# Row-tiled matmuls of an attention kernel, paired by pass: two scores side by side, then both halves of a maximum unit

## The reference

```python
xn = layernorm(x)
k, q, v = split(xn @ W_kqv.T)                      # 8 batches, 16 heads, 1024 tokens, 16 columns
score = einsum('bhsd,bhnd->bhsn', q, k) / 16 + bias
out_attn = softmax(score) @ v
result = x + out_attn + ffn(xn)
```

## Time and profile before

| what | value |
|---|---|
| time, median of 3 runs | 2495.86 us (2490.36 to 2496.33) |
| time of the profiled execution | 2484.07 us |
| its span | 2482.3 us |
| mean granted TensorE clock | 0.98 |
| busy: PE, DVE, ACT, POOL | 97%, 77%, 63%, 31% of the span |
| PE matmul instructions | 19286 |
| first maximum matmul, first score matmul | 1106.3 us, 1143.0 us |
| first score matmul of the last group | 2436.45 us |

### The profile page before, as it was taken

How to read it: one execution, slowest core, us unless ns; L and a number is a source line. 1 busy time by engine, 2 the same in 40 slices (tenths; PEclk the granted TensorE clock), 3 DMA queues, 4 the chain that set the end, 5 groups by cost and what they waited for, 6 DMA issues and landing times.

```text
span 2482.3 us, 53369 instructions
## 1 busy us (share of the span) xinstructions
PE 2396.7 (97%) x19286; PEld 1475.7 (59%) x19286; DVE 1910.9 (77%) x2905; ACT 1561.7 (63%) x3212; POOL 781.2 (31%) x901
## 2 busy tenths in 40 slices
PE   6999999994999999988999999999999999999998
PEld 5888888884999999973333333333333333333333
DVE  5666666656556555559999999999999999999994
ACT  3333333333333333324888888888888888888888
POOL 2223332224342222220113333333333333333333
PEclk9999999996999999987999999999999999999999
DMA  6999978880232222234434344343434353535331
GB/s 187 169 165 160 184 139 145 137 127 27 80 95 75 75 76 76 72 70 72 70 62 88 76 77 81 75 83 71 86 70 86 69 90 65 90 66 92 63 58 42
DMA packets 177922, 229.01 MB, mean 92 GB/s; under 512 B 42828, under 2 KB 127436, under 8 KB 177656
## 3 DMA queue, kind: packets, MB, share of 16 engines
q1 hardware_dynamic: 153048, 172.02, 38.6%
q0 software_dynamic: 22448, 50.56, 8.7%
q10 hardware_dynamic: 2176, 3.02, 0.3%
HBM read 131.47 MB, written 93.66 MB: 91 GB/s over the span
## 4 chain that ended last, share of the span: by engine, by line
PE 53%; DVE 1%; DMA 0%; ACT 0%; issue 0%; SPq 0%; DVEq 0%
PE p_o L1399 23%; PE p L1389 19%; PE p L1376 9%; PE p L1409 1%; DVE part L1231 1%; PE p L1382 1%; DMA q_op<-m_row 0%; ACT probs L1351 0%; ACT o_sb L1339 0%; SPq L1120 0%; DVE neg L1239 0%; DVE att L1258 0%; DVE att L1278 0%; DVE rec L1255 0%; DVEq L1224 0%
## 5 line engine op out<-in xcount | busy, mean ns | idle before, releaser
L1231 DVE TENSOR_REDUCE part<-p 128x2 f32<-128x1024 f32 x1024 | 1243.2, 1221 | 73.8 <-PE p L1376 66.7
L1351 ACT ACTIVATE probs<-p 128x512 f32<-128x512 f32 x2048 | 1112.6, 597 | 162.1 <-PE p L1389 131.0
L1376 PE MATMUL p<-k_op,q_op 50*128 50x512 f32 x2048 | 759.4, 462 | 13.9 <-DVE part L1231 10.9
L1389 PE MATMUL p<-q_op,k_op 51*128 51x512 f32 x2048 | 758.6, 452 | 0.9 <-DVE part L1231 0.4
L1399 PE MATMUL p_o<-probs,v_op 128*32 128x256 f32 x8192 | 655.5, 392 | 4.5 <-ACT o_sb L1339 0.8
L1389 PEld LDWEIGHTS p<-q_op,k_op 51*128 51x128 f32 x2048 | 311.2, 185 | 417.8 <-ACT probs L1351 374.3
L1399 PEld LDWEIGHTS p_o<-probs,v_op 128*32 128x32 f32 x8192 | 163.7, 108 | 359.3 <-ACT probs L1351 305.8
L1376 PEld LDWEIGHTS p<-k_op,q_op 50*128 50x128 f32 x2048 | 304.3, 189 | 29.4 <-DVE part L1231 26.2
L1182 POOL TENSOR_TENSOR att<-o_t,rec 128x256 f32<-128x256 f32 x63 | 39.0, 619 | 810.9 <-DVE rec L1247 810.9
L809 POOL DMA_INDIRECT xe<-xn_scratch,ids x135 | 144.4, 1070 | 361.4 <-DMA ids<-lists_scratch 345.6
L902 ACT ACTIVATE gated_e<-p_gate 128x352 f32<-128x352 f32 x135 | 62.6, 464 | 190.7 <-PE p_gate L840 190.7
(11 more groups left out here) (178 smaller groups left out, 4046.7 us busy)
## 6 DMA issues: line engine op xcount, KB each, us to landing
k_op<-qk_scratch SPq DMA_DIRECT2D x192, 128.0 KB
q_op<-qk_scratch SPq DMA_DIRECT2D x192, 128.0 KB
yr_scratch<-y SPq DMA_DIRECT2D x135, 128.0 KB, 1.7
qk_scratch<-k_op SPq DMA_DIRECT2D x32, 512.0 KB
qk_scratch<-q_op SPq DMA_DIRECT2D x32, 512.0 KB
v_scratch<-v_op SPq DMA_DIRECT2D x16, 1024.0 KB, 15.5
v_op<-v_scratch SPq DMA_DIRECT2D x32, 512.0 KB, 9.9
x<-in_x SPq DMA_DIRECT2D x16, 512.0 KB, 4.3
```

The source lines that it names most:

```text
L1231: v.tensor_reduce(part[c_ % 2][:, kh, :, qb], p1[use % 2][:], AX.X, ALU.max, negate=True).then_inc(s["s1_read"], 1)
L1351: a.activation(probs[kb % 4][:, h], p2[use % 3][:], ACT.Exp).then_inc(s["s2_read"], 1)
L1376: return t.matmul(p1[use % 2][:, x], q_op[u][lo:lo + S1_ROWS, pair, q0:q0 + P], k_op[u][lo:lo + S1_ROWS, pair, kh * 512:(kh + 1) * 512], s ...
L1389: t.matmul(p2[use % 3][:], k_op[u][lo:lo + S2_ROWS, pair, kb * P:(kb + 1) * P], q_op[u][lo:lo + S2_ROWS, pair, half * HQ:(half + 1) * HQ], ...
```

## The change

Both scores of a step are issued together at odd n, and behind them both halves of the maximum unit. No instruction is added or removed. The step becomes score(n-1), x=0 | score(n), x=1 | max_half x=0 | max_half x=1 | products. The score with x = 1 is now second in the order and the wait for it moves with it; the wait on `s1_read` moves from the head of the step to a place behind both scores. The prologue is left as it is.

```diff
@@ -1432,14 +1432,15 @@
                     if n == 0:
                         pe.wait_ge(v_in[u], (turn + 1) * 16)
                     use, use1 = use2(g, n), ring1(g) + n // 2
-                    pe.wait_ge(s["s2_read"], use + 1)
-                    if has_next and n % 2 == 0:
-                        pe.wait_ge(s["s1_read"], use1 + 1)
-                    score(u, use, n)
+                    if n % 2:
+                        for m in (n - 1, n):
+                            pe.wait_ge(s["s2_read"], use2(g, m) + 1)
+                            score(u, use2(g, m), m)
                     if has_next:
-                        ins = max_half(nu, use1, n // 2, 1 - n % 2)
                         if n % 2:
-                            ins.then_inc(s["s1_ps"], 1)
+                            pe.wait_ge(s["s1_read"], use1 + 1)
+                            max_half(nu, use1, n // 2, 0)
+                            max_half(nu, use1, n // 2, 1).then_inc(s["s1_ps"], 1)
                         if n == TURN_AT:
                             turn_max(g + 1, 0, use + 1)
                     if n == OWN_TURN:
```

## The result

| | median | runs |
|---|---|---|
| before | 2493.84 us | 5, 2490.36 to 2496.33 |
| after | 2506.55 us | 5, 2503.19 to 2510.34 |
| after / before | 1.0057 | 95% interval 1.0043 to 1.0071 |

The change costs 0.57%, some 14 us (the two medians differ by 12.7). It was predicted as 16.7 us on top of the kernel before (2512.6 us against a median of 2495.86), within 2491 to 2540.

The account below looks back on a forecast made before the run. The prediction took PE to bound the kernel, with DVE close behind. Terms of 14.6, 1.8 and about 0.3 us made 16.7 us on the median of 2495.86: 2512.6 us, range 2491 to 2540.

Parts of the forecast that it names:

- PE is the bound, so its loss counts in full: Attention: PE bounds the chain, so a slower PE adds its whole loss; a faster one gains at most 63 us.
- The pairing costs and gains nothing: Ordinary steps: score beside score, maximum beside maximum run like mixed pairs; 0, bounds 0.01 us a step either way.
- The first rival: All 992 steps: alternating order starts second pairs up to 0.10 us earlier, DVE then bounds; 2433 us; chance 0.08.
- The rule of the Trainium skill: Weight loads: one overlaps matmuls in flight only when its row group differs, favouring the new order; counted as 0.
- The late step: Step of l=6 and 7: second score waits for its buffer, products 0.24 us later, 61 times, 14.6 us.
- The step of l = 16 and 17: Step behind the output transpose: second score waits for the first exponential; 0.03 us, 61 times, 1.8 us.
- The slack of 0.06 us in ordinary steps: Ordinary steps: second score could start 0.06 us before the step does, so its earlier wait costs 0.
- the second rival: Ordinary steps lack the slack: exponential 0.03 us late in 930 steps, 28 us more, 2541 us; chance 0.13.
- The total: Whole kernel: the step losses together add 16.7 us, all on PE, giving 2512.6 us against the median.
- The 0.3 us for the first group: Second step of the first group: a buffer is waited for there too, about 0.3 us.
- only neighbours in the order pair up: Matmuls on the array: taken for granted that only neighbours in program order run side by side; no size given.

Follow-up runs that it names:

- the early transpose: Transpose of maxima moved from l=5 to behind the products of l=3: 2489.85 us on the kernel before, 2495.21 us on the changed kernel.
- the first four runs above: Changed kernel, old order at l=6,7: 2486.99 us; old order, second score's wait first: 2511.84; transpose of maxima at l=9: new order 2508.44, old order 2497.71.
- the first experiment: Changed kernel with the old order restored only in the step of l=6 and 7: 2486.99 us, 0.9986 of the kernel before.

## Why the prediction was right

*PE is the bound, so its loss counts in full.* It did: DVE's wait for PE grew by 15.3 us and attention by 17.0.

*The pairing costs and gains nothing.* Ordinary steps are 1.235 to 1.240 us, with the loads where they were forecast, 0.11 us into the step. The first rival (faster) needed loads that start sooner, and there were none to start sooner. The rule of the Trainium skill (TensorE: Matmul & The Clock Gate, Part 3, "What overlaps and what doesn't"), weighed in the prediction, would by the first rival's working have made a step up to 0.10 us shorter; no run here shows it. The run with both scores on one half goes against the rule: its second loads are on the rows of the matmuls in flight, and its step is 1.233 us all the same.

*The late step.* Predicted 0.24 us, measured 1.567 - 1.329 = 0.238. With 61 of them that is 14.5 us of the 17.0. Four runs bear on its cause: the wait alone, moved in the old order, brings it; the old order in that one step takes it away; a transpose in another place of the buffer ring makes it smaller; and the old waits with two matmuls left on the late score's rows bring it too.

*The step of l = 16 and 17.* Predicted 0.03, measured 0.021: 1.3 us instead of 1.8.

*What I had not counted.* Six single steps of the table's places l = 12, 13 and l = 0, 1 were longer by 0.17 to 0.69 us, 2.1 us in all, and one of l = 4, 5 by 0.16. In each that I looked at, ACT started an exponential late though its score was done. The longest:

```profile
1348.76 0.50 PE L1389 MATMUL p<-q_op,k_op 51*128 51x512 f32 x1
1349.45 0.50 PE L1389 MATMUL p<-q_op,k_op 51*128 51x512 f32 x1 [0.19 <-ACT probs L1351]
```

```profile
1348.80 0.60 ACT L1351 ACTIVATE probs<-p 128x512 f32<-128x512 f32 x1 [0.90 <-PE p L1389]
```

```profile
1348.88 1.23 DVE L1231 TENSOR_REDUCE part<-p 128x2 f32<-128x1024 f32 x1 [0.58 <-PE p L1376]
```

DVE started its reduction late at the same moment (its matmuls end at 1348.26), so it isn't ACT alone that was held up. The kernel before shows three longer steps, of 1.30 to 1.44 us. The slack of 0.06 us in ordinary steps is real: in the profile after, the first exponential ends 0.10 us ahead of the next step, and PE answers 0.04 behind it. A disturbance beyond the slack now falls on PE in full, where the old order covered some 0.24 us of it (its late step lost 0.09 for a load 0.33 late). Two runs show both costs: with the early transpose, the step of l = 0 and 1 in the middle of groups 1 to 4 (n = 32 and 33) is 1.40 to 1.43 us in the old order and 1.53 to 1.57 in the new one. This is the second rival in a mild form, 2 us instead of 28, and only part of it is the change's doing. The disturbance isn't made by the order: the profiles of the first four runs above show none of these four steps. What it is stays open.

*The total.* That the sum hit 16.7 against 17.0 in attention is in part luck. The 0.3 us for the first group didn't come (from its first score to its products at n = 31 it is 22.47 us before, 22.44 after), the prologue, which the change leaves alone, was 0.6 us shorter in this execution, and against that stand the steps that were not counted. The medians moved by less, 12.7 us. The late step alone is measured tightly, 61 times over.

*A picture that was wrong without harm.* I took it that only neighbours in the order pair up. By the runs on rows, each half of the array works through its own matmuls. What costs in the late step is that a wait holds back everything behind it for both halves, and that a maximum half has to follow the late score on the score's own rows. In the old order the late matmul was the last on its rows, and the other half had its first one done.

## What to carry to other kernels

Where one engine issues in order, a wait should stand as late as it can, and the matmul that may come late should be the last on its part of the array: the same four matmuls cost 0.24 us more in the late step where one wait moved forward. Before a piece of work is moved, look for what else waits in its old place: the transpose of maxima filled a hole that another wait made, and away from there it cost 0.21 us a time. When the bound engine looks evenly busy, compare the lengths of the same step over all rounds; here one step in sixteen held nearly all of the loss.

## What the runs showed of the hardware that was not expected

- A matmul can start ahead of one that stands before it in the program, if that one needs rows that are busy and its own rows are free (score 1 passing maximum 0 in the run with scores and maxima on the same rows: starts at 1908.87 and 1909.19). It did not pass an unmet wait: in the changed kernel the maximum half x = 0 starts at 1935.92, with the late score.
- With all matmuls of K = 50 or 51 on one half of the array the granted clock stayed at 0.50 (1.2 GHz) through 3 ms of attention with PE busy 100%. In the run with scores on one half and maxima on the other it was 1.00 in the same stretch (1226 to 1850 us), and in the kernels before and after it rose to 1.00 some 9 us after the scores began. So at the level of this kernel, work on both halves is worth the clock as well as the places: 0.92 of 1.77 us a step. Why the clock stays down is not shown.
- Ordinary steps come in two lengths, 1.227 and 1.240 us, and nearly every half keeps to one or the other (not in two runs: 1.233 in all with scores on one half of the array, 1.236 to 1.241 with maxima first). In the first experiment they alternate from half to half (20.71 and 20.83 us for a half), while the kernel before has the shorter in 7 of 60 halves and the changed one in 11. That is some 4 us over attention and may be why that run came out under before; what sets it stays open.
